# Root mean square in the narrow layers: from a column of sums, Pool's power and a turn to a full tile of sums with Ln and Exp on ScalarE

## The reference

```python
def rmsnorm(x, w, eps=EPS):
    xf = x.astype(jnp.float32)
    inv = jax.lax.rsqrt(jnp.mean(xf * xf, axis=-1, keepdims=True) + eps)
    return (xf * inv).astype(x.dtype) * w
xn = rmsnorm(x, norm_w)
q = (xn @ wq).reshape(B, T, N_HEADS, HEAD_DIM)
...
attn = jax.nn.softmax(scores.astype(jnp.float32), axis=-1).astype(q.dtype)
out = jnp.einsum('bgrts,bsgd->btgrd', attn, v).reshape(B, T, N_HEADS * HEAD_DIM)
return residual + out @ wo
```

## Time and profile before

| | |
|---|---|
| time before, median of 3 runs | 1790.3 us (1779.28 to 1790.84) |
| the profiled execution, its own time | 1784.43 us |
| its span in the profile | 1782.6 us |
| PE busy | 92% |
| DVE busy | 68% |
| ACT busy | 57% |
| POOL busy | 26% |
| mean granted clock of PE | 0.962 of full |

### The profile page before, as it was taken

One profiled execution on the slowest core, in us unless ns is written; L12 is line 12 of the kernel. 1 busy time (PEld: TensorE's weight loads), 2 busy tenths in 40 slices (PEclk: granted clock), 3 DMA queues, 4 the chain that ended last, 5 costly groups with the idle time before them and its releaser, 6 DMA issues.

```text
span 1782.6 us, 29688 instructions
## 1 busy us (share of the span) xinstructions
PE 1640.6 (92%) x10732; PEld 883.1 (50%) x10732; DVE 1219.0 (68%) x2339; ACT 1022.8 (57%) x1737; POOL 461.3 (26%) x325
## 2 busy tenths in 40 slices
PE   6899568999999999999999999999999999999785
PEld 5787333444444545454545453545444545454442
DVE  4474546677867777777866777677777877686651
ACT  2111145566666676667675766567666767666452
POOL 4342301123222131313131323122222222232212
PEclk9998779999999999999999999999999999999987
DMA  8987631050215121522235122512150316121322
GB/s 281 325 276 251 159 107 38 25 107 25 64 33 127 28 80 34 106 44 75 74 95 123 44 80 68 102 28 81 40 122 26 80 38 122 30 77 26 120 68 79
DMA packets 177459, 165.30 MB, mean 93 GB/s; under 512 B 91802, under 2 KB 133146, under 8 KB 175778
## 3 DMA queue, kind: packets, MB, share of 16 engines
q1 hardware_dynamic: 175010, 152.91, 33.0%
q10 hardware_dynamic: 2304, 10.49, 1.5%
HBM read 117.73 MB, written 45.58 MB: 92 GB/s over the span
## 4 chain that ended last, share of the span: by engine, by line
PE 50%; issue 11%; DVE 10%; SPq 6%; POOL 6%; ACT 3%; DMA 3%; POOLq 0%; ACTq 0%; DVEq 0%
PE general L1584 9%; PE general L1470 9%; PE score_ps L1524 5%; PE score_ps L1525 5%; PE out_ps L1540 4%; POOL kept L1346 4%; PE general L1485 3%; PE general L1489 3%; SPq L1022 3%; PE score_ps L1513 2%; DVE q_aux L1378 2%; PE out_ps L1560 2%; DVE q_pair L1379 2%; DVE q_pair L1380 2%; PE sum_ps L1544 2%
## 5 line engine op out<-in xcount | busy, mean ns | idle before, releaser
L1390 DVE TENSOR_REDUCE tops<-general 128x2 bf16<-128x308 f32 x1024 | 434.8, 471 | 111.0 <-PE general L1485 60.4
L1238 ACT ACTIVATE probs<-score_ps 128x512 f32<-128x512 f32 x512 | 298.1, 598 | 153.0 <-PE score_ps L1525 140.0
L1346 POOL TENSOR_TENSOR kept<-kept,inv_b 128x512 f32<-128x512 f32 x128 | 168.0, 1334 | 461.8 <-DMA inv_b<-scratch_inverses 461.8
L1377 DVE CAST q_aux<-q_pair 64x512 bf16<-64x512 f32 x160 | 87.6, 548 | 197.6 <-ACT q_pair L1226 196.6
L1248 ACT ACTIVATE q_aux<-general 4x512 bf16<-4x512 bf16 x320 | 187.3, 585 | 39.1 <-PE general L1496 33.3
L1225 ACT ACTIVATE q_pair<-general 64x512 fp32r<-64x512 f32 x160 | 94.5, 590 | 133.3 <-PE general L1470 132.2
L1334 POOL TENSOR_TENSOR x_lo<-xn,x_hi 128x1024 fp32r<-128x1024 f32 x32 | 75.8, 2370 | 319.3 <-ACT x_hi L1206 187.6
L1485 PE MATMUL general<-w_top,q_aux 128*128 128x154 bf16 x1024 | 134.7, 239 | 23.2 <-DVE q_pair L1380 15.4
L1525 PE MATMUL score_ps<-q_pair,w_pair 128*128 128x512 f32 x256 | 150.4, 594 | 0.0
L1403 DVE TENSOR_TENSOR a_lo<-kept,a_hi 128x512 fp32r<-128x512 f32 x160 | 120.0, 783 | 44.2 <-ACT a_hi L1285 43.3
L1285 ACT ACTIVATE a_hi<-kept 128x512 fp32r<-128x512 f32 x160 | 93.6, 625 | 96.9 <-PE general L1584 43.3
(11 more groups left out here) (149 smaller groups left out, 3310.2 us busy)
## 6 DMA issues: line engine op xcount, KB each, us to landing
inv_b<-scratch_inverses SPq DMA_DIRECT2D x128, 256.0 KB, 4.8
xn<-scratch_stream SPq DMA_DIRECT2D x16, 512.0 KB, 3.4
w_pair<-scratch_wk_hi SPq DMA_DIRECT2D x32, 256.0 KB
x<-scratch_stream SPq DMA_DIRECT2D x16, 512.0 KB, 3.3
inv_n<-scratch_inverses SPq DMA_DIRECT2D x256, 32.0 KB, 1.8
scratch_stream<-x SPq DMA_DIRECT2D x14, 512.0 KB, 4.4
scratch_wk_hi<-p_kout_hi SPq DMA_DIRECT2D x16, 308.0 KB
p_raw<-in_L_xattn_Wk_dram SPq DMA_DIRECT2D x4, 1024.0 KB, 7.6
```

The costliest lines, as they stand in the source:

```text
L1238: nc.scalar.activation(dst, score_ps[:, number % 2, :], ACT.Exp, scale=scale).then_inc(act_exp.sem, 1)
L1346: last = nc.gpsimd.tensor_tensor(tiles[i], tiles[i], (inv_b, inv_n)[n % 2][:, i, :], ALU.mult)
L1390: last = nc.vector.tensor_reduce(tops[:, n % 2, sub, 2 * pair:2 * pair + 2], src, AX_X, ALU.max)
```

## The change

The sum over channels now has the ones as its weights, a full 128 by 128 tile of them, and the squares as the moving operand of 512 tokens. So each partition of the result holds the sums of all tokens, already spread. ACT reads that bank with Ln (scale 1/256, bias EPS from a tile `eps`), writes `root`, and takes the exponential of -0.5 times that. `rate` on DVE reads `root`. DVE's `meansq`, POOL's power and PE's turns in `rate` are gone, and with them one use of a bank. Separately, `tops` has now 128 columns for each 128 tokens, of which 4 are written and the others cleared at the start, so that a turn of maxima has 128 columns of weights instead of 4.

```diff
-GENERAL = [(*x, m) for x in PLAN if x[1] in ("query", "max", "turn", "output", "square", "rate", "give")
+GENERAL = [(*x, m) for x in PLAN if x[1] in ("query", "max", "turn", "output", "square", "give")
...
-        tops = sb("tops", [P, 2, 4, 4], BF16)
-        meansq, rate, power = sb("meansq", [P, 4]), sb("rate", [P, 4]), sb("power", [P, 4])
-        ident, ident_bf, ones = sb("ident", [P, P]), sb("ident_bf", [P, P], BF16), sb("ones", [P, 1])
+        tops = sb("tops", [P, 2, 4, P], BF16)
+        root, eps = sb("root", [P, TOK]), sb("eps", [P, 1])
+        ident, ident_bf, ones = sb("ident", [P, P]), sb("ident_bf", [P, P], BF16), sb("ones", [P, P])
...
         reader = {"query": dve_query, "max": dve_max, "turn": act_turn, "output": dve_output,
-                  "square": dve_square, "rate": dve_rate, "give": act_give}
+                  "square": act_mean, "give": act_give}
...
+                elif what == "square":
+
+                    wait(act, pe_square.sem, pe_square.after(it, what, n, k))
+                    wait(act, dve_rate.sem, dve_rate.after(*rate_before(it, n)))
+                    nc.scalar.activation(root[:], bank_of((it, what, n, k, 0)), ACT.Ln, bias=eps[:], scale=1.0 / C).then_inc(act_mean.sem, 1)
+                    wait(act, act_mean.sem, act_mean.after(it, what, n, k))
+                    nc.scalar.activation(root[:], root[:], ACT.Exp, scale=-0.5).then_inc(act_root.sem, 1)
...
-                elif what == "square":
-                    wait(pool, dve_square.sem, dve_square.after(it, what, n, k))
-                    nc.gpsimd.tensor_tensor(rate[:], meansq[:], power[:], ALU.pow).then_inc(pool_rate.sem, 1)
...
-            for buf in (w_top, q_aux, w_aux, w_aux_rest, n_aux, n_aux_rest):
+            for buf in (w_top, q_aux, w_aux, w_aux_rest, n_aux, n_aux_rest, tops):
...
-                elif what == "square":
-                    wait(dve, pe_square.sem, pe_square.after(it, what, n, k))
-                    last = nc.vector.tensor_scalar(meansq[:], bank_of((it, what, n, k, 0))[:, 0:4], 1.0 / C, EPS, ALU.mult, ALU.add)
-                    last.then_inc(dve_square.sem, 1)
                 elif what == "rate":
 
-                    wait(dve, pe_rate.sem, pe_rate.after(it, what, n, k))
-                    ps = bank_of((it, what, n, k, 0))
+                    wait(dve, act_root.sem, act_root.after(it, "square", n, k))
                     for m in range(KC):
-                        last = nc.vector.tensor_tensor(xn[:, m, :], ps, x[:, HALF[n], m, :], ALU.mult)
+                        last = nc.vector.tensor_tensor(xn[:, m, :], root[:], x[:, HALF[n], m, :], ALU.mult)
...
-                        last = nc.tensor.transpose(ps[0:4].bitcast(BF16)[:, sub * P:(sub + 1) * P], tops[:, n % 2, sub, :], ident_bf[:])
+                        last = nc.tensor.transpose(ps.bitcast(BF16)[:, sub * P:(sub + 1) * P], tops[:, n % 2, sub, :], ident_bf[:])
...
-                    for sub in range(4):
-                        for c in range(KC):
-                            last = nc.tensor.matmul(ps[:, sub:sub + 1], xn[:, c, sub * P:(sub + 1) * P], ones[:],
-                                                    start=(c == 0), stop=(c == KC - 1))
+                    for c in range(KC):
+                        last = nc.tensor.matmul(ps, ones[:], xn[:, c, :], start=(c == 0), stop=(c == KC - 1))
...
-                elif what == "rate":
-                    wait(pe, pool_rate.sem, pool_rate.after(it, "square", n, k))
-                    ps = bank((it, what, n, k, 0))
-                    for sub in range(4):
-                        last = nc.tensor.transpose(ps[:, sub * P:(sub + 1) * P], rate[:, sub:sub + 1].to_broadcast([P, P]), ident[:])
-                    last.then_inc(pe_rate.sem, 1)
```

More of the change, by code:

```diff
@@ L870, in layers @@
         sum_ps = ctx.enter_context(nc.psum_tensor("sum_ps", [P, 512], F32))
-        ROWS_CLEARED, CLEARED = 6, 9
+        ROWS_CLEARED, CLEARED = 7, 9
         WIDE_QUERY, KEY_ROWS, WIDE_OUT = 16 * 2, 16 * 8, 16 * 2
@@ L894, in layers @@
         pe_score, pe_value = signal("pe_score", "rest", "score"), signal("pe_value", "value")
-        pe_output, pe_square, pe_rate = signal("pe_output", "output", times=KC), signal("pe_square", "square"), signal("pe_rate", "rate")
+        pe_output, pe_square = signal("pe_output", "output", times=KC), signal("pe_square", "square")
         act_split, act_query, act_exp = signal("act_split", "split", "rate"), signal("act_query", "query"), signal("act_exp", "rest", "score")
@@ L902, in layers @@
         dve_output = signal("dve_output", "output", times=KC)
-        dve_square, dve_rate = signal("dve_square", "square"), signal("dve_rate", "rate")
-        pool_split, pool_rate = signal("pool_split", "split", "rate"), signal("pool_rate", "square")
+        act_mean, dve_rate = signal("act_mean", "square"), signal("dve_rate", "rate")
+        pool_split, act_root = signal("pool_split", "split", "rate"), signal("act_root", "square")
         pool_parts = Signal(sem("pool_parts"), ("scale",), only=(1, 3))
@@ L935, in last_query, with rate_before @@
             return (before_w, "query", 4 * before + 3, 1) if before % 2 == 0 else (before_w, "query", 4 * before + 2, 0)
+        rates = [(w, n) for w, what, n, k in PLAN if what == "rate"]
+        def rate_before(w, n):
+            at = rates.index((w, n))
+            w, n = rates[at - 1] if at else (-1, 0)
+            return w, "rate", n, 0
         def bank_of(use):
@@ L1298, in _ @@
                                     pattern=[[-1, P]], channel_multiplier=1).then_inc(ident_ready, 1)
-            nc.gpsimd.memset(power[:], -0.5).then_inc(ident_ready, 1)
+            nc.gpsimd.memset(eps[:], EPS).then_inc(ident_ready, 1)
             pool.wait_ge(ident_ready, 3)
```

## The result

The changed kernel takes 1793.4 us in the median of 20 runs (1786.5 to 1799.5), the kernel before, run beside it, 1786.0 us (1775.1 to 1793.7). The ratio is 1.0049 with a 95% interval of 1.0035 to 1.0063: 8.7 us slower, half a per cent. On the 1790.3 us of the prediction the ratio gives 1799 us, inside the range and 12 us under the number.

The account below looks back on a forecast made before the run. Around each narrow chunk DVE behind ACT was taken to set the pace, PE following with little slack. 14.4 (ACT) + 6 (clock) + 0.5 (clearing) = 20.9 us; on the median 1790.3 the forecast is 1811 us, range 1789 to 1838.

Parts of the forecast that it names:

- The credit for what was removed: Narrow chunks: removing DVE's meansq, POOL's power and PE's rate turns gains zero while DVE leads; about 10 us if PE led.
- The squares on PE: Sum over channels, narrow chunks: two full-width matmuls take 1.7 to 2.0 us against 1.75; no difference taken, upper end 4 us.
- ACT, 14.4 us: Sixteen narrow chunks: Ln, exposed second load, Exp and displaced exponential start `q_pair` 0.9 us later each, 14.4 us in all.
- no doubled load: Rival at ACT's loads: each costs twice its row, 2.8 us a place, 45 us, about 1855 us; chance 0.12.
- 0.1 us, gone in ACT's backlog: PE's query after the squares waits 0.1 us for Ln to free the bank of the sums; no cost counted.
- The clock, 6 us: After PE's longer stops at narrow chunks the clock halves: four drops at 1.5 us, 6 us; ends none and 27 us.
- PE so stands about 1.8 us instead of 0.66: PE's wait at narrow chunks grows to about 1.8 us, in one piece at the eight places of chunk 3.
- The turns of maxima, 0 us: 128 turns on PE, now with 128 columns of weights: at most 2 us from longer weight loads, taken as zero.
- the clearing of `tops`: At the kernel's start, before the loads of masks and keys that wait for it: adds 0.5 us.
- its own upper terms: Upper ends: 14.4 us ACT's delay, 27 clock drops at all sixteen places, 0.5 clearing at the start, 4 squares on PE.
- ACT's delay is covered: Rival, between the sums and `q_pair`: slack hides the delay, 1781 to 1797 us; chance 0.14 within 1%, 0.04 over 1% faster.
- the held clock: Rival at PE's stops: they stay short enough, the clock holds, only 14.4 + 0.5 is lost, 1805 us; chance 0.25.

Follow-up runs that it names:

- experiments 5 and 6: 5: changed kernel with the root left out, DVE only adding epsilon to the mean, 0.9985; 6: the same, DVE reading 4 of 512 columns, mean left out too, 0.9966.
- Experiments 3 to 6: 3: changed kernel with one table set holding Ln and Exp loaded once at the start, 1780.8 us, 0.9974; the others: see experiment 4 and experiments 5 and 6.
- experiment 4: Changed kernel with one more table load (the set of Ln) at each of the sixteen places, between Ln and the load for Exp; 1815.4 us, ratio 1.0189.

## Why the prediction was off

**The credit for what was removed: zero, right.** With the turn of the rate and POOL's power gone and nothing on ACT in their place (experiments 5 and 6), the kernel is no faster than with the turns alone (0.9985 and 0.9966 against 0.9941 and 0.9952). PE only waits where it worked.

**The squares on PE: no difference, right.** 1.76 us against 1.75.

**ACT, 14.4 us: right in its working and nearly in its size.** Forecast 0.9 us a place, seen 0.84 at `q_pair` and 0.80 at the narrow query (15.90 against 15.10), 13 us in all; the first load hidden, the second not; no doubled load. Ln was longer than its row by 0.09 us (0.69 against 0.60). Experiments 3 to 6 split the 0.84: 0.56 us are the second load, as far as ACT's idle time doesn't cover it, and 0.28 are the wait of PE's query for Ln, which the prediction called "0.1 us, gone in ACT's backlog". It was 0.24 us at the query, and once the load is gone it is the delay that is left.

**The clock, 6 us: not the term that failed, but its picture of the place was wrong.** "PE so stands about 1.8 us instead of 0.66" in one piece, at the chunks 3, was 1.53 us and, behind more work, 0.53; and the window behind has a clock of 1.00. The size is another matter. In the mean over all executions the clock stands 0.0028 lower than in the kernel before. An estimate from the runs: if PE were the limit all the time, that is 5 us of 1786; over the 67 executions of the kernel before that lie beside the experiments, one with 0.001 less clock took 1.06 us longer in the mean, which makes it 3 us. Only the kernels with a load in the open have less clock (0.9620, 0.9623 with the root alone, 0.9550 with one load more); all the others that were run more than once lie between 0.9642 and 0.9660. So 3 to 5 us were lost where 6 were forecast; at which places isn't shown.

**The turns of maxima, 0 us: the step that failed, and made the number wrong.** "A weight load of 4 columns takes 84 ns, one of 128 columns 99 ns" prices the load, and what the change touched was the distance to the neighbours. It is worth 8.6 to 10.5 us (two measurements; their intervals reach from 4 to 14 us). Counted along PE's timeline, 16 turns stand between two queries and gain 0.20 us each, 46 between a query and a value and gain 0.08 (in 0.09 less, out 0.01 more), 12 between an output and a score 0.17, 9 between narrow maxima 0.19, 5 between wide maxima and a score 0.15: 11.4 us in all for these 88 of the 128 turns, of which some lies ahead of waits. The exit to a value in the earlier trace rows couldn't tell: it is 0.32 us, and 0.33 with 128 columns. But the entry was to be seen in the trace of before, and a turn between two queries, 0.32 in and 0.31 out where a query follows a query after 0.23, stands in it 16 times. The prediction bounded this term from above only, by 2 us, and not from below.

**The sum again.** 13 us for ACT and 3 to 5 for the clock, less 8.6 to 10.5 for the turns, in which the clearing of `tops` (0.48 us in the trace) is contained: 5 to 10 us, and 8.7 were measured. With the turns at what they are worth the forecast would have been 10 to 12 us slower and not 20.7. (Its range ended at 1838 us, 2 us above what its own upper terms, 14.4, 27, 0.5 and 4, add up to.)

**The rivals.** The measured 1793.4 us lies in the band of "ACT's delay is covered" (1781 to 1797 us), the 1799 us on the prediction's own base 2 us above it, and both are within the 1% that this rival shared with the held clock. But it isn't so by its mechanism: nothing was covered. A right reading of the time alone would have taught the wrong lesson.

**What stays open.** The local delay is 13 us in all, and the root alone cost 19.3 (16.0 to 22.6). Its clock is 0.9623 in the mean against 0.9646 beside it, by the same estimate 2 to 4 us, which brings the sum to 15 to 18 us, in the lower part of the interval. One more stop was found behind it. In the tenth narrow chunk DVE's casts came late enough in the kernel with the root alone to meet POOL's scaling. DVE, POOL and PE there:

```profile
1193.76 2.69 POOL L1358 TENSOR_TENSOR kept<-kept,inv_n 128x512 f32<-128x512 f32 x2 [5.09 <-DMA inv_n<-scratch_inverses]
1194.04 1.28 DVE L1389 CAST q_aux<-q_pair 64x512 bf16<-64x512 f32 x1 [1.62 <-ACT q_pair L1241]
1195.33 1.41 DVE L1390 CAST q_aux<-q_pair 64x512 bf16<-64x512 f32 x1
...
1198.21 0.81 PE L1496 MATMUL general<-n_top,q_aux 128*128 128x308 bf16 x3 [0.83 <-DVE q_pair L1392]
```

In the kernel before, the first of the two casts took 0.42 us and was over before POOL went on, the second began at 1190.83 and took 0.42 too, and PE didn't stop here:

```profile
1190.40 0.42 DVE L1377 CAST q_aux<-q_pair 64x512 bf16<-64x512 f32 x1 [1.62 <-ACT q_pair L1226]
...
1191.12 2.51 POOL L1346 TENSOR_TENSOR kept<-kept,inv_n 128x512 f32<-128x512 f32 x2 [5.04 <-DMA inv_n<-scratch_inverses]
```

Whether such meetings are more frequent with the root on ACT, or only elsewhere, wasn't tried; over the whole run the two casts together take no longer (548 and 592 ns in the mean before, 537 and 599 with the root alone), which speaks for elsewhere.

## What to carry to other kernels

When a change touches the shape of a small operation on PE, don't price the operation but the distance from its predecessor and to its successor, and look in the trace for a place where it stands between two full ones. Before putting two functions on ACT, count the loads and see whether one set holds both: here one line was worth 13 us. When a change has two halves, run each alone: a small total can be two large terms. And take the clock from all executions and not from the one that has a trace: here the traced ones showed it higher after the change, the mean of all shows it lower.

## What the runs showed of the hardware

- A matmul that writes fewer than 128 columns beside one that writes all 128 costs PE 0.08 to 0.09 us on the way in (0.32 to 0.33 us start to start from a query, against 0.24) and 0.11 to 0.14 on the way out (0.31 to 0.34 to a query, against 0.20), with 4, 32 and 64 columns alike.
- A turn of 64 columns and the matmuls of 64 columns behind it run side by side: 0.14 us start to start, 0.33 with 128 or 32.
- A table load is 1283 ns, with no further pause around it: in the changed kernel the second load starts at 1063.10, where Ln ends at 1063.09, and Exp 0.02 us behind the load's end. The sixteen loads that experiment 4 adds take 1283 ns too; by the name that is asked for they load again the set which Ln has just used, though the trace doesn't name sets. The page "ScalarE: Activation LUTs" of the Trainium skill (section "What ACT_TABLE_LOAD costs") adds 1380 ns of drain to each switch; no run here shows it, and in these two rows there is no room for it.
- DVE's cast of 64x512 from SBUF to SBUF takes 0.42 us alone and up to 1.41 us while POOL runs a tensor-tensor, whereas the tensor-tensor out of PSUM keeps its 0.68 us beside it (1191.29 in the kernel before, under POOL's 1191.12).
